# An expert stage's loads moved to SyncE, and one subtraction to GpSimd

## The chip, the cores and the metric

The kernel runs on one core of a Trainium2 chip. The time is that of the device for one launch, in microseconds (us). The core's engines are TensorE (PE; its weight loads are listed as PEld), VectorE (DVE), ScalarE (ACT), GpSimd (POOL) and SyncE (SP), each with its own instruction stream, joined by semaphores. A transfer (DMA) is issued by an engine's queue and done by 16 DMA engines that all queues share.

## The reference

Eight images of 256 channels and 1024 positions go through three layers. The first two are attentions with eight heads; the third, which the change touches, is a layer of 32 experts, computed densely: every expert for every token, with a weight that is zero for all but a token's two best experts.

```python
sel = jax.nn.sigmoid(xt @ expert_sel.T)
sel_val, sel_idx = jax.lax.top_k(sel, TOP_K)                  # TOP_K = 2
w = jnp.zeros((T, E)).at[jnp.arange(T)[:, None], sel_idx].add(sel_val)
h = jax.nn.relu(jnp.einsum('td,edh->teh', xt, keys))          # E = 32, d = 256, H = 64
out = jnp.einsum('teh,te,ehv->tv', h, w, values)
t = t + out.reshape(B, S, -1)
```

## The kernel before

The work is a list of steps per image, written out by hand in `Steps`; every engine walks the same list and does its own part of each step. The sections are `first`, `head`, `body` (a loop of seven) and `last`. The body computes image n's two attentions and, at its beginning, the expert layer of image n-1, its steps spread among the score tiles ("top" steps) of image n. `last` holds the expert layer of the eighth image with nothing beside it. So there are eight expert stages.

All products of this layer are made in float32 accuracy from three float32r products: each operand is split into an upper part (a cast on ScalarE) and a lower part (the value minus its upper part).

A stage handles two halves of 512 tokens (`hf`) and, in each, 16 pairs of experts (`j`, `ET = 16`, `EPT = 2` experts of 64 hidden rows make 128 partitions), so m = 16 hf + j runs over 32 "experts" (pairs). For each m:

- `load_expert(m)` brings keys and values, 128 rows of 2 KB, into `expert_sb[:, m % 4]`; `load_gates(m)` brings the two experts' rows of gates, each repeated over 64 partitions, into `gate_bc[:, m % 4]` (in `probs`). Both are issued by GpSimd (L486, L491), in a ring of four.
- ScalarE casts the keys (L806), GpSimd subtracts their lower part (L498), both two experts ahead.
- TensorE makes 6 matmuls of 512 columns into `ps_one` ("up", L540 to L542).
- VectorE makes the gated activation, relu(up) x gate, into `gated` (L1151).
- ScalarE casts it (L931, `gated_hi`) and casts the values (L932); GpSimd subtracts the values' lower part (L498); VectorE subtracts the activation's lower part (`lower`, L970), one expert later: after the gated activation of m+1.
- TensorE makes 6 matmuls of the values with the activations into `ps_acc`, two experts later (`times_down`). At each half's end the step "down" adds the sum to `x_res` on VectorE (L1160) and SyncE stores it.

GpSimd's order for expert m is: lower part of the keys m+2, of the values m, wait for that result, issue weights m+4, wait until the bank of m-1 was read, issue gates m+3. The two waits are these:

```python
if m + RING < NH * ET:
    hold(vals_down, "up", m + 1)
    load_expert(m + RING)
if 1 <= m and m - 1 + RING < NH * ET:
    b, n = sec.bank(("up",) + divmod(m - 1, ET))
    hold(bank_read[b], b, n)
    load_gates(m - 1 + RING)
```

The gates come from the step "logits" (VectorE), are turned by TensorE ("turn"), copied to `w_turn` (L1141), stored by SyncE to DRAM (`gates_dram`, eight transfers, L435) and only then loaded back. SyncE's other work is the stacks (L424: queries and keys copied into the attention's layout, 12 transfers for each "stack" step), the next image's load and the stores of the output. In the body, between "logits" and "turn", there is one group of stacks; another comes just before "logits". A score tile costs TensorE two matmuls (L657) and VectorE one maximum over 1024 columns (L1055).

Of the kernel before, what the change touches and what calls it, by code (L numbers as in the profile page):

```python
# [46 lines left out]
class Steps:  # L47
# [49 lines left out]
    def experts_of(self, tops):  # L97

        ups = [("up", hf, j) for hf in range(self.halves) for j in range(self.experts)]
        steps = spread(ups, tops) if tops else ups  # L100
        at = steps.index(("up", 0, self.experts - 1)) + 1
        behind = at + 2 if tops else at
        return steps[:at] + [("lower", 0)] + steps[at:behind] + [("down", 0)] + steps[behind:] + [("lower", 1)]

    def batch(self, experts):
        tops = rows_later(self.top(0, 0, 0) + self.top(0, 0, 1) + self.top(0, 1, 0) + self.top(0, 1, 1))
# [76 lines left out]
def bass_hybrid_kernel(nc: bass.Bass, x, mats, vecs, norm_wb, sel_t, experts, out, w_dram):  # L183
# [76 lines left out]
    with ExitStack() as ctx:  # L260
# [3 lines left out]
        def sem(name):  # L264
            return ctx.enter_context(nc.semaphore(name))
# [57 lines left out]
        ps_acc = ctx.enter_context(nc.psum_tensor("ps_acc", [P, 2, HALF], F32))  # L323

        passed = sem("passed")
        passed_too = sem("passed_too")
        consts = sem("consts")
        fills = sem("fills")
        weights_in = sem("weights_in")
# [44 lines left out]
        def f(ap):  # L374
            return ap.bitcast(F32)
# [12 lines left out]
        @block.sync  # L388
        def _(sp):
            sp.dma_start(x_in[:, :, :], x[0].rearrange("(k p) t -> p k t", p=P)).then_inc(x_loaded, 16)  # L390
            sp.dma_start(probs[:, :, :, :].rearrange("p a g t -> p (a g t)"),
                         mats.rearrange("p m k c -> p (m k c)")).then_inc(weights_in, 16)
            sp.dma_start(bias[:, :, :], vecs).then_inc(weights_in, 16)
            sp.dma_start(gnw[:, :, :], norm_wb).then_inc(weights_in, 16)
            sp.dma_start(sel_w[:, :, :], sel_t).then_inc(weights_in, 16)

            def emit(sec, it):
                def hold(semaphore, kind, n, each=1):

                    sp.wait_ge(semaphore, sec.value(kind, n, each))  # L400
                    sp.sem_inc(passed, 1)

                def read(u):
                    b, n = sec.bank(u)
                    hold(bank_read[b], b, n)

                for s in sec.steps:
                    if s[0] == "stack":
                        _, st, g, hf = s

                        read(("qk", st, g, "q", hf))
                        read(("qk", st, g, "k", hf))

                        if st:
                            hold(acc_read, "acc", sec.no["acc"][("norm", 0, g, NH - 1)])
                        elif g == 0 and sec.name != "first":
                            hold(acc_read, "acc", sec.no["acc"][("norm", 1, g, NH - 1)])
                        elif sec.name == "body":
                            hold(acc_read, "acc", 0)
                        for j in range(G):  # L420
                            rows = slice(HD * j, HD * j + HD)

                            for quad, pair in enumerate(stacked_pairs(j)):
                                sp.dma_start(f(stacks[HD * quad:HD * quad + HD, :, g, j, half(hf)]),  # L424
                                             f(nat[rows, pair, half(hf)])).then_inc(stacked[g][hf][j], 16)
                    if s == ("out", 0, NH - 1, CT - 1):

                        read(s)
                        sp.dma_start(x_in[:, :, :],
                                     x[bass.ds(next_batch(it, B), 1)].rearrange("a (k p) t -> p (a k) t", p=P)  # L430
                                     ).then_inc(x_loaded, 16)
                    if s[0] == "turn":
                        read(s)
                        for i in range(TT):
                            sp.dma_start(w_dram[:, P * i:P * i + P],  # L435
                                         w_turn[E * (i % PH):E * (i % PH) + E, i // PH, :]).then_inc(gates_out, 16)
                    if s[0] == "down":
                        hf = s[1]
                        hold(acc_read, "acc", sec.no["acc"][s])
                        where = out[B - 1:B] if sec.name == "last" else out[bass.ds(it - 1, 1)]  # L440
                        sp.dma_start(where.rearrange("a (k p) t -> p (a k) t", p=P)[:, :, half(hf)],
                                     x_res[:, :, half(hf)]).then_inc(stored[hf], 16)

            run(sp, emit)
            last = Section("last")
            sp.wait_ge(gates_out, last.value("turn", 1, 16 * TT))
            for hf in range(NH):
                sp.wait_ge(stored[hf], last.value("turn", 1, 16))
# [3 lines left out]
        def _(pool):  # L452
# [24 lines left out]
                               channel_multiplier=-1).then_inc(consts, 1)  # L477

            def emit(sec, it):
                def hold(semaphore, kind, n, each=1):  # L480

                    pool.wait_ge(semaphore, sec.value(kind, n, each))
                    pool.sem_inc(passed_too, 1)

                def load_expert(m):
                    pool.dma_start(expert_sb[:, m % RING, :], experts[m % ET]).then_inc(expert_in[m % RING], 16)  # L486

                def load_gates(m):
                    hf, j = divmod(m, ET)
                    row = w_dram[EPT * j:EPT * j + EPT, half(hf)]  # L490
                    pool.dma_start(gate_bc[:, m % RING, :],  # L491
                                   bass.AP(row.tensor, row.offset, [[T, EPT], [0, H], [1, HALF]])
                                   ).then_inc(gate_in[m % RING], 16)

                def lower(m, upper_parts, parts, c, lowered):

                    pool.wait_ge(upper_parts, sec.value("up", m + 1))
                    pool.tensor_tensor(parts[:, 2 + m % 2, :], expert_sb[:, m % RING, c:c + C],  # L498
                                       f(parts[:, m % 2, :]), ALU.subtract).then_inc(lowered, 1)

                for s in sec.steps:
                    if s[0] == "logits":

                        hold(acc_read, "acc", 0)
                        for m in range(RING):
                            load_expert(m)
                    if s[0] == "inputs":
                        pool.wait_ge(acts_hi, sec.value("acts", sec.no["acts"][s]))
                        pool.tensor_tensor(act_lo[:, :, :], xn[:, :, :], f(act_hi[:, :, :]),
                                           ALU.subtract).then_inc(acts_lo, 1)  # L510
                    if s[0] == "turn":
                        for m in range(2):
                            lower(m, keys_up, keys_parts, 0, keys_down)
                        hold(gates_out, "turn", sec.no["turn"][s], 16 * TT)
                        for m in range(RING):
                            load_gates(m)
                    if s[0] == "up":
                        m = s[1] * ET + s[2]
                        if m + 2 < NH * ET:
                            lower(m + 2, keys_up, keys_parts, 0, keys_down)  # L520
                        lower(m, vals_up, vals_parts, C, vals_down)
                        if m + RING < NH * ET:

                            hold(vals_down, "up", m + 1)
                            load_expert(m + RING)
                        if 1 <= m and m - 1 + RING < NH * ET:

                            b, n = sec.bank(("up",) + divmod(m - 1, ET))
                            hold(bank_read[b], b, n)
                            load_gates(m - 1 + RING)  # L530

            run(pool, emit)

# [407 lines left out]
        def _(dve):  # L941
# [12 lines left out]
            def emit(sec, it):  # L954
# [9 lines left out]
                def done(ins, u):  # L964
                    ins.then_inc(bank_read[sec.bank(u)[0]], 1)

                def lower(m):

                    dve.wait_ge(gated_up, sec.value("up", m + 1))
                    dve.tensor_tensor(gated_lo[:, m % 2, :], gated[:, m % RING, :], f(gated_hi[:, m % 2, :]), ALU.subtract).then_inc(gated_down, 1)  # L970

                links = [0]

                def link(ins):
# [12 lines left out]
                for s in sec.steps:  # L987
# [154 lines left out]
                    elif kind == "up":  # L1142
# [1 line left out]
                        m = hf * ET + j  # L1144
                        acc = full(s)
                        r = m % RING
                        dve.wait_ge(gate_in[r], (sec.value("turn", 0) * (NH * ET // RING) + m // RING + 1) * 16)

                        if m >= RING:
                            dve.wait_ge(gated_down, sec.value("up", m + 1 - RING))  # L1150
                        done(dve.scalar_tensor_tensor(out=gated[:, r, :], in0=acc, scalar=0.0,  # L1151
                                                      in1=gate_bc[:, r, :], op0=ALU.max, op1=ALU.mult), s)
                        if j:
                            lower(m - 1)
                    elif kind == "lower":
                        lower((s[1] + 1) * ET - 1)
                    elif kind == "down":
                        hf = s[1]
                        dve.wait_ge(downed, sec.value("up", (hf + 1) * ET))
# [58 lines left out]
```

## Time and profile before

| | |
|---|---|
| median of 3 runs | 4135.63 us (4131.19 to 4144.11) |
| the profiled execution | 4131.6 us, its span 4129.9 us |
| TensorE busy | 3465.9 us, 84% of the span |
| VectorE, ScalarE | 2018.6 us, 1666.6 us |
| GpSimd | 767.5 us |
| mean granted TensorE clock | 0.88 |

The span is the time from the first to the last instruction of one profiled execution; the time beside it is that execution's own. Rows of stretches (Rows 2 below) give start and end, length, busy us and instructions of PE, PEld, DVE, ACT and POOL, then the mean granted clock, the DMA engines' busy share and GB/s; the sums add up stretches.
### The profile page before, as it was taken

The numbers are of one execution on the slowest core, as the hardware profiler recorded it, in microseconds if no ns is written. First come the engines' busy times: TensorE is split into PE (matmuls) and PEld (weight loads), VectorE is DVE, ScalarE is ACT, GpSimd is POOL, SyncE is SP. The second block draws the span as 40 slices with busy tenths as digits, with TensorE's granted clock in tenths as the row PEclk, the third lists the DMA queues.
The fourth block names the chain that finished last, engine by engine and source line by source line (L and its number), as shares of the span: only waits on it lengthen the run. The fifth ranks groups of instructions, "written<-read, shape, count | busy, mean of one in ns | idle before, by whom it ended". The sixth has DMA issues, their size and how long they took to land.

```text
span 4129.9 us, 54399 instructions
## 1 busy us (share of the span) xinstructions
PE 3465.9 (84%) x18386; PEld 1874.5 (45%) x18386; DVE 2018.6 (49%) x2825; ACT 1666.6 (40%) x2604; POOL 767.5 (19%) x1051
## 2 busy tenths in 40 slices
PE   5898789887898878988789888898789987898866
PEld 2344554435534455344554445443454434544444
DVE  6435572355724566245652556434563345733533
ACT  1453335442363423634236342453334543355322
POOL 0000260003500044000530005300152001610035
PEclk7797899988998889979899788997889978999889
DMA  3011440214402143022420224211341113411134
GB/s 92 1 42 31 105 119 15 57 25 110 114 12 52 40 115 97 16 57 51 111 77 16 57 66 112 61 31 42 78 111 49 42 31 90 118 32 41 31 89 117
DMA packets 229742, 263.78 MB, mean 64 GB/s; under 512 B 137424, under 2 KB 139472, under 8 KB 229328
## 3 DMA queue, kind: packets, MB, share of 16 engines
q1 hardware_dynamic: 73808, 124.88, 12.6%
q0 software_dynamic: 155648, 135.17, 12.6%
q8 instruction: 170, 2.79, 0.3%
q14 instruction: 116, 0.95, 0.1%
HBM read 145.80 MB, written 9.44 MB: 38 GB/s over the span
## 4 chain that ended last, share of the span: by engine, by line
PE 51%; DVE 14%; DMA 12%; issue 10%; ACT 7%; SPq 2%; POOL 2%; DVEq 0%; ACTq 0%; POOLq 0%
PE ps_acc L588 9%; DMA probs<-gates_dram 9%; PE ps_two L693 8%; PE ps_acc L597 8%; DVE tops L1055 7%; PE ps_one L540 4%; PE ps_one L542 3%; PE ps_one L541 3%; PE ps_two L657 3%; PE ps_one L693 3%; DMA expert_sb<-experts_dram 3%; POOL nat L498 2%; SPq L424 2%; ACT probs L862 1%; ACT stacks L845 1%
## 5 line engine op out<-in xcount | busy, mean ns | idle before, releaser
L1055 DVE TENSOR_REDUCE tops<-ps_two 128x2 bf16<-128x1024 f32 (+3 forms) x896 | 963.0, 1110 | 414.6 <-PE ps_two L657 245.2
L862 ACT ACTIVATE probs<-ps_two 128x1024 f32<-128x1024 f32 (+1 forms) x704 | 642.7, 961 | 302.3 <-PE ps_two L693 229.1
L657 PE MATMUL ps_two<-stacks 32*128 32x512 f32 (+3 forms) x1792 | 444.1, 522 | 254.2 <-DVE tops L1055 200.1
L486 POOL DMA_DIRECT2D expert_sb<-experts_dram x256 | 142.8, 560 | 2593.6 <-DVE rsum L1069 2459.5
L693 PE MATMUL ps_two<-stacks 97*128 97x512 f32 (+3 forms) x1408 | 469.4, 445 | 61.9 <-ACT probs L862 33.5
L588 PE MATMUL ps_acc<-probs,v_sb 128*32 128x512 f32 (+3 forms) x3584 | 475.4, 605 | 0.0
L597 PE MATMUL ps_acc<-probs,ones 128*32 128x512 f32 (+3 forms) x3584 | 448.5, 574 | 0.0
L806 ACT CAST nat<-expert_sb 128x256 fp32r<-128x256 f32 x256 | 103.1, 405 | 850.2 <-DVE probs L1151 604.7
L498 POOL TENSOR_TENSOR nat<-expert_sb,nat 128x256 fp32r<-128x256 f32 x512 | 376.9, 740 | 371.3 <-ACT nat L806 279.6
L657 PEld LDWEIGHTS ps_two<-stacks 32*128 32x128 f32 x1792 | 178.2, 208 | 546.4 <-DVE tops L1055 307.2
L693 PEld LDWEIGHTS ps_two<-stacks 97*128 97x128 f32 x1408 | 253.8, 199 | 335.4 <-issue 189.6
L1151 DVE SCALAR_TENSOR_TENSOR probs<-ps_one,probs 128x512 f32<-128x512 f32 x256 | 176.3, 689 | 371.1 <-issue 170.1
L1069 DVE COPY rsum<-ps_acc 128x512 f32<-128x512 f32 x64 | 44.2, 690 | 551.8 <-PE ps_acc L597 551.8
L540 PE MATMUL ps_acc<-nat 128*128 128x512 f32 x512 | 225.2, 440 | 68.8 <-DVE nat L970 66.7
L540 PE MATMUL ps_one<-act_hi,nat 128*128 128x512 f32 x512 | 242.7, 474 | 28.5 <-POOL nat L498 28.5
L862 ACT ACTIVATE probs<-ps_one 128x512 f32<-128x512 f32 (+3 forms) x384 | 170.0, 488 | 193.6 <-PE ps_one L697 100.8
L845 ACT CAST stacks<-ps_two 1x1024 fp32r<-1x1024 f32 x128 | 128.6, 1005 | 266.1 <-PE ps_two L674 263.5
L540 PE MATMUL ps_one<-act_hi,w_hi 128*128 128x512 f32 x392 | 179.9, 459 | 45.6 <-DVE act_lo L1037 16.9
L541 PE MATMUL ps_one<-act_lo,nat 128*128 128x512 f32 x512 | 217.6, 425 | 0.0
L542 PE MATMUL ps_one<-act_hi,nat 128*128 128x512 f32 x512 | 217.3, 424 | 0.0
L491 POOL DMA_DIRECT2D probs<-gates_dram x256 | 209.0, 819 | 41.6 <-DMA gates_dram<-w_turn 17.6
L597 PEld LDWEIGHTS ps_acc<-probs,ones 128*32 128x32 f32 x3584 | 114.1, 116 | 223.4 <-issue 216.3
(129 smaller groups left out, 4754.5 us busy)
## 6 DMA issues: line engine op xcount, KB each, us to landing
stacks<-nat SPq DMA_DIRECT2D x792, 128.0 KB, 2.4
expert_sb<-experts_dram POOLq DMA_DIRECT2D x256, 256.0 KB, 5.5
probs<-gates_dram POOLq DMA_DIRECT2D x256, 256.0 KB, 8.7
x_in<-x_in_dram SPq DMA_DIRECT2D x9, 1024.0 KB, 4.9
out_dram<-x_res SPq DMA_DIRECT2D x16, 512.0 KB, 4.2
probs<-mats_dram SPq DMA_DIRECT2D x1, 2048.0 KB, 9.4
gates_dram<-w_turn SPq DMA_DIRECT2D x64, 16.0 KB, 1.6
sel_w<-sel_dram SPq DMA_DIRECT2D x1, 32.0 KB, 8.5
```

The lines of the kernel that those rows point to most:

```text
L491: pool.dma_start(gate_bc[:, m % RING, :], bass.AP(row.tensor, row.offset, [[T, EPT], [0, H], [1, HALF]])).then_inc(gate_in[m % RING], 16)
L498: pool.tensor_tensor(parts[:, 2 + m % 2, :], expert_sb[:, m % RING, c:c + C], f(parts[:, m % 2, :]), ALU.subtract).then_inc(lowered, 1)
L540: pe.matmul(acc, lh, rh, start=start, stop=False)
L541: pe.matmul(acc, lh, rl, start=False, stop=False)
L542: return pe.matmul(acc, ll, rh, start=False, stop=stop)
L588: pe.matmul(ps_acc[HD * j:HD * j + HD, 0, a:HALF], v_sb[:, k, c:c + HD], probs[:, sec.no["mix"][s] % 2, j, a:HALF], start=(k == 0), stop=( ...
L597: mm = pe.matmul(ps_acc[HD * j:HD * j + HD, 1, a:HALF], ones32[:], probs[:, sec.no["mix"][s] % 2, j, a:HALF], start=(k == 0), stop=(k == l ...
L657: mm = pe.matmul(acc[:, HALF * e:HALF * e + n_keys], q_st[rows, g, j, P * i:P * i + P], k_st[rows, g, j, HALF * kh:HALF * kh + n_keys], st ...
L693: mm = pe.matmul(at[:, a:HALF], k_st[0:MID + 1, g, j, P * k:P * k + P], q_st[0:MID + 1, g, j, HALF * hf + a:HALF * hf + HALF], start=True, ...
L862: done(act.activation(probs[:, n % 2, per * i:per * i + per, a:HALF], acc[:, :, a:HALF], ACT.Exp, scale=SCALE), s + (i,))
L1055: done(dve.reduce_max(tops[:, kh, 2 * pr:2 * pr + 2, i], acc[:, :, 0:cols(st, i, kh)], AX_X), s)
L1151: done(dve.scalar_tensor_tensor(out=gated[:, r, :], in0=acc, scalar=0.0, in1=gate_bc[:, r, :], op0=ALU.max, op1=ALU.mult), s)
```

## The change

It has three parts. The loads of weights and gates are issued by SyncE, not by GpSimd, with the waits that they need; in SyncE's order the gates m+3 stand ahead of the wait for the values of m. A gate load is made of two transfers, one for each of the two rows of gates, and what waits for it counts both. The lower part of the gated activation is subtracted by GpSimd, last in its order for an expert, and no longer by VectorE.

```diff
@@ Steps.experts_of
-        return steps[:at] + [("lower", 0)] + steps[at:behind] + [("down", 0)] + steps[behind:] + [("lower", 1)]
+        return steps[:behind] + [("down", 0)] + steps[behind:]
@@ SyncE, emit
+                def load_expert(m):
+                    sp.dma_start(expert_sb[:, m % RING, :], experts[m % ET]).then_inc(expert_in[m % RING], 16)
+                def load_gates(m):
+                    hf, j = divmod(m, ET)
+                    for n in range(EPT):
+                        row = w_dram[EPT * j + n:EPT * j + n + 1, half(hf)]
+                        sp.dma_start(gate_bc[H * n:H * n + H, m % RING, :],
+                                     bass.AP(row.tensor, row.offset, [[0, H], [1, HALF]])
+                                     ).then_inc(gate_in[m % RING], 16)
...
+                    if s[0] == "logits":
+                        hold(acc_read, "acc", 0)
+                        for m in range(RING):
+                            load_expert(m)
+                    if s[0] == "up":
+                        m = s[1] * ET + s[2]
+                        if 1 <= m and m - 1 + RING < NH * ET:
+                            read(("up",) + divmod(m - 1, ET))
+                            load_gates(m - 1 + RING)
+                        if m + RING < NH * ET:
+                            hold(vals_down, "up", m + 1)
+                            load_expert(m + RING)
...
+                        hold(gates_out, "turn", sec.no["turn"][s], 16 * TT)
+                        for m in range(RING):
+                            load_gates(m)
@@ GpSimd, emit
-                def load_expert(m):
-                    pool.dma_start(expert_sb[:, m % RING, :], experts[m % ET]).then_inc(expert_in[m % RING], 16)
-                def load_gates(m):
-                    hf, j = divmod(m, ET)
-                    row = w_dram[EPT * j:EPT * j + EPT, half(hf)]
-                    pool.dma_start(gate_bc[:, m % RING, :],
-                                   bass.AP(row.tensor, row.offset, [[T, EPT], [0, H], [1, HALF]])
-                                   ).then_inc(gate_in[m % RING], 16)
...
                         lower(m, vals_up, vals_parts, C, vals_down)
-                        if m + RING < NH * ET:
-                            hold(vals_down, "up", m + 1)
-                            load_expert(m + RING)
-                        if 1 <= m and m - 1 + RING < NH * ET:
-                            b, n = sec.bank(("up",) + divmod(m - 1, ET))
-                            hold(bank_read[b], b, n)
-                            load_gates(m - 1 + RING)
+                        pool.wait_ge(gated_up, sec.value("up", m + 1))
+                        pool.tensor_tensor(gated_lo[:, m % 2, :], gated[:, m % RING, :], f(gated_hi[:, m % 2, :]),
+                                           ALU.subtract).then_inc(gated_down, 1)
@@ VectorE, emit
-                        dve.wait_ge(gate_in[r], (sec.value("turn", 0) * (NH * ET // RING) + m // RING + 1) * 16)
+                        dve.wait_ge(gate_in[r], (sec.value("turn", 0) * (NH * ET // RING) + m // RING + 1) * 16 * EPT)
...
-                        if j:
-                            lower(m - 1)
-                    elif kind == "lower":
-                        lower((s[1] + 1) * ET - 1)
```

GpSimd's waits and loads at the steps "logits" and "turn" go as well.

## Rows read from the trace of the kernel before

**Rows 1.** The page: the chain of work that ended last, by engine and line.

```profile
PE ps_acc L588 9%; DMA probs<-gates_dram 9%; PE ps_two L693 8%; PE ps_acc L597 8%; DVE tops L1055 7%; PE ps_one L540 4%; PE ps_one L542 3%; PE ps_one L541 3%; PE ps_two L657 3%; PE ps_one L693 3%; DMA expert_sb<-experts_dram 3%; POOL nat L498 2%; SPq L424 2%; ACT probs L862 1%; ACT stacks L845 1%
```

**Rows 2.** Stretches: a body stage, seven body stages, seven starts, last start, last stage.

```profile
991.32:1143.86 152.54, 131.10 (x540) 86.05 (x540) 107.29 (x129) 47.50 (x102) 84.08 (x118) 0.91 0.39 104
...
sum 1057.74, PE 914.53 PEld 604.96 DVE 748.07 ACT 332.44 POOL 588.50; mean PE 130.65 PEld 86.42 DVE 106.87 ACT 47.49 POOL 84.07
...
sum 126.46, PE 68.38 PEld 35.43 DVE 52.28 ACT 4.97 POOL 55.41; mean PE 9.77 PEld 5.06 DVE 7.47 ACT 0.71 POOL 7.92
...
3975.72:3990.50 14.78, 4.06 (x12) 2.93 (x12) 0.42 (x1) 0.00 (x0) 3.72 (x5) 0.73 0.22 53
3990.50:4125.20 134.70, 99.13 (x372) 71.92 (x372) 42.84 (x66) 39.04 (x94) 84.75 (x118) 0.94 0.47 117
```

**Rows 3.** The chain in the last stage, in order of time (start, us, what).

```profile
4013.80 0.70 DVE probs L1151
...
4014.53 0.41 ACT nat L806
4014.93 0.52 ACT nat L931
4015.46 0.32 ACT nat L932
...
4015.84 0.74 POOL nat L498
...
4027.04 0.70 DVE probs L1151
```

**Rows 4.** The page's DMA issues: KB each, median us from issue to landing.

```profile
stacks<-nat SPq DMA_DIRECT2D x792, 128.0 KB, 2.4
expert_sb<-experts_dram POOLq DMA_DIRECT2D x256, 256.0 KB, 5.5
probs<-gates_dram POOLq DMA_DIRECT2D x256, 256.0 KB, 8.7
```

**Rows 5.** Timeline of a body step between two gated activations (start, length).

```profile
1049.61 0.68 DVE L1151 SCALAR_TENSOR_TENSOR probs<-ps_one,probs 128x512 f32<-128x512 f32 x1
...
1050.95 2.36 DVE L1055 TENSOR_REDUCE tops<-ps_two 128x2 bf16<-128x1024 f32 x2
...
1051.40 0.40 PE L541 MATMUL ps_one<-act_lo,nat 128*128 128x512 f32 x1
...
1053.22 0.68 DVE L1151 SCALAR_TENSOR_TENSOR probs<-ps_one,probs 128x512 f32<-128x512 f32 x1
...
1053.72 0.39 PE L542 MATMUL ps_acc<-nat 128*128 128x512 f32 x1
```

**Rows 6.** Waits in a body stage: us in total, times, longest.

```profile
ACT nat L806 <- DMA expert_sb<-experts_dram: 24.5, 6, 5.6
DVE probs L1151 <- DMA probs<-gates_dram: 19.8, 8, 10.2
PEld ps_two L657 <- DVE tops L1055: 17.3, 11, 6.8
```

**Rows 7.** The stacks' transfers on SyncE: ns min/median/max of an issue.

```profile
L424 SPq DMA_DIRECT2D stacks<-nat x792: 585/597/1976, 37.0 to 3960.1; - x198
```

**Rows 8.** DMA from 983.2 to 1000, mostly gate loads: packets, queue share.

```profile
DMA packets 2456, 1.59 MB, mean 95 GB/s; under 512 B 2072, under 2 KB 2072, under 8 KB 2456
...
q0 software_dynamic: 2456, 1.59, 35.1%
```

**Rows 9.** DMA from 924 to 930: four weight loads, two stacks.

```profile
DMA packets 319, 1.05 MB, mean 175 GB/s; under 512 B 63, under 2 KB 63, under 8 KB 319
...
expert_sb<-experts_dram POOLq DMA_DIRECT2D x4, 256.0 KB, 3.6
```

**Rows 10.** GpSimd's two subtractions by form: count, busy, mean ns.

```profile
L498 POOL TENSOR_TENSOR nat<-expert_sb,nat 128x256 fp32r<-128x256 f32 x512 | 376.9, 740 | 371.3 <-ACT nat L806 279.6 <-ACT nat L932 73.1
...
L509 POOL TENSOR_TENSOR act_lo<-xn,act_hi 128x2048 fp32r<-128x2048 f32 x8 | 36.0, 4503 | 348.5 <-ACT act_hi L912 348.5
```

More of the change, by code:

```diff
@@ L325, in bass_hybrid_kernel @@
         passed = sem("passed")
-        passed_too = sem("passed_too")
         consts = sem("consts")
@@ L479, in emit @@
             def emit(sec, it):
-                def hold(semaphore, kind, n, each=1):
-                    pool.wait_ge(semaphore, sec.value(kind, n, each))
-                    pool.sem_inc(passed_too, 1)
-                def load_expert(m):
-                    pool.dma_start(expert_sb[:, m % RING, :], experts[m % ET]).then_inc(expert_in[m % RING], 16)
-                def load_gates(m):
-                    hf, j = divmod(m, ET)
-                    row = w_dram[EPT * j:EPT * j + EPT, half(hf)]
-                    pool.dma_start(gate_bc[:, m % RING, :],
-                                   bass.AP(row.tensor, row.offset, [[T, EPT], [0, H], [1, HALF]])
-                                   ).then_inc(gate_in[m % RING], 16)
                 def lower(m, upper_parts, parts, c, lowered):
@@ L501, in emit @@
                 for s in sec.steps:
[L502 to L506, printed above, removed]
                     if s[0] == "inputs":
@@ L513, in emit @@
                             lower(m, keys_up, keys_parts, 0, keys_down)
-                        hold(gates_out, "turn", sec.no["turn"][s], 16 * TT)
-                        for m in range(RING):
-                            load_gates(m)
                     if s[0] == "up":
@@ L965, in done @@
                     ins.then_inc(bank_read[sec.bank(u)[0]], 1)
-                def lower(m):
-                    dve.wait_ge(gated_up, sec.value("up", m + 1))
-                    dve.tensor_tensor(gated_lo[:, m % 2, :], gated[:, m % RING, :], f(gated_hi[:, m % 2, :]), ALU.subtract).then_inc(gated_down, 1)
                 links = [0]
```

## The prediction

> **What bounds the kernel now.** I read the page's chain first, then the time by stage, then the chain inside the expert stage, then the waits and the DMA. The chain of work that ended last is mostly TensorE's lines, but 9% of the span, as much as for any line, go to one kind of transfer, the gate loads (`probs<-gates_dram`), and 3% to the weight loads [rows 1]. The change touches only the expert stages, so the question is how much of the time they are, and what they wait for.
>
> There are eight: seven in the loop body, interleaved with the attention's score tiles ("tops"), and one alone at the end. The seven last 1057.7 us from the first gated activation (L1151) to the first half's output sum, 151.1 us each; the last takes 134.7. Ahead of each lies a start, from the copy of the turned gates (L1141) to that first activation: 126.5 us in seven, 18.1 each, and 14.8 in the last [rows 2]. Together 1334 of 4130 us. TensorE's granted clock is 0.91 in a body stage, a mixture of its two levels, 2.4 and 1.2 GHz. In the last stage VectorE is busy for 43 us of 134.7, GpSimd for 85: neither is full, so something is waited for.
>
> What it is shows in one link of the last stage's chain: gated activation m, three copies on ScalarE, GpSimd's subtraction for the values, two issues, the gate load, gated activation m+3. That is 4027.04 - 4013.80 = 13.24 us for three experts, 4.41 per expert; the work in it is 0.70 + 0.41 + 0.52 + 0.32 + 0.74 = 2.7, all else is issuing and landing [rows 3], and a gate load lands 8.7 us after its issue [rows 4]. The weights make a second loop of nearly the same length, over two experts: copies 0.41, 0.52 and 0.32, GpSimd 0.74, about 1.1 to the end of the issue, landing 5.5: 8.6, or 4.3 per expert [rows 3, 4]. Relieving one of the two alone would give little.
>
> A body stage is a mixture. Two gated activations with two tiles between them stand only 3.61 us apart where nothing is late [rows 5]; the mean over the stage is 4.6. In one stage ScalarE stands 24.5 us for weights and VectorE 19.8 for gates (10.2 of that before the first activation), and TensorE 17.3 for VectorE's maxima, which queue behind the late gated activations [rows 6].
>
> **The gate load leaves GpSimd, as two rows.** 256 issues go from GpSimd; 512 come to SyncE, and 256 of the weights. A stack transfer takes SyncE 0.60 us to issue [rows 7], so 1.8 us per expert, under any period here (0.3 each would make 0.9, 1.5 each 4.5). Landing: 8.7 us now for 256 KB; a SyncE transfer of 128 KB, which a row is too, lands in 2.4 [rows 4]. The trace shows no broadcast row on SyncE; bounds are 2.4 and 8.7, and I take 3.0, near the transfer of the same size and queue. What speaks for it: today's gate loads are odd. In a stretch that is mostly gate loads 2072 of 2456 packets are under 512 B [rows 8], and in one with four weight loads and two stacks 63 of 319 [rows 9]. A plain row has no reason for them.
>
> The Trainium skill ("DMA: Bandwidth & Descriptors", Rules for kernel authors) says that an outermost dimension of c < 16 confines a DMA to at most c engines, here two. The 16 engines are busy for 35.1% of that stretch on this queue [rows 8], which two of them could not give (13%): the trace does not agree. By the rule a row would spread over eight times the engines, by the row of the trace it only loses small packets; the sum takes 3.0 either way.
>
> **The order on SyncE.** For expert m SyncE waits for the bank of m-1, issues gates m+3 (two rows), waits for the values' subtraction of m, issues weights m+4. Gates m+3 are now asked for right after the values of m-1, a period earlier: 3 us after gated activation m-1, and with 1.8 of issues and 3.0 of landing that is 7.8 us, wanted after four periods (12 us or more). Even 8.7 would be in time: the gate loop is gone. What is late next is the weight loop, 0.41 + 0.52 + 0.32 + 0.74 + 0.1 + 0.6 = 2.7 plus the landing L, over two experts. L is 5.5 now, but 3.6 where weights go without gates [rows 9]. With L = 3.0 (between 2.4 for half the bytes and 5.5) it is 2.85 per expert; with 5.5 it stays at 4.1. Behind a waiting SyncE stand only more loads and the half's store; the stacks are issued before the stage. The four first weight loads (2.4 us of issues) go between two groups of stacks, while TensorE still computes what the second group copies. Taken as nothing; without that cover 2.4 in each of eight batches, 19 in all.
>
> **The start.** The first gate load lands 8.7 us after its issue; then two issues and a landing, 1.2 + 3.0 = 4.2. I take a gain of 4.3 in each of eight starts (0 to 5).
>
> **The subtraction moves from VectorE to GpSimd.** GpSimd's price for 128x512 is not in the trace: 0.74 us for 256 columns and 4.50 for 2048 [rows 10] make 2.1 ns a column, so 1.28 (between those two ends). GpSimd then needs 0.74 + 0.74 + 1.28 + 0.1 = 2.86 per expert, without issues; VectorE loses one 128x512 subtraction per expert. The lower part comes last in GpSimd's order, behind the next keys' and the values' subtraction, some 2.5 us later after its activation than now. The product that needs it runs two experts later, which hides that; at the two "down" steps nothing does, so +1 us at the first, where tiles follow, and +3 at the stage's end.
>
> **The sum.** Last stage: TensorE goes from one matmul to the next in 0.23 us at full clock (ten steps from 1051.40 to 1053.72 [rows 5]), 12 of them make 2.76; GpSimd 2.86, weights 2.85. With three limits so close I take 3.05: 31 x 3.05 = 94.6, 4.5 for the end, 3 for low clock: 102 for 134.7. Gain 33, with the start 37.
>
> Body stage: TensorE is the bound. A step with two tiles is 3.61; less 2.76, a tile is 0.43. 31 x 2.76 = 85.6; 54 tiles (64 of the plan less the ten ahead of the stage) x 0.43 = 23.2; seven turns of the row maxima, 0.9 each, an estimate from a tile's 0.43 and a wait as long, 6.3; both ends 4: 119. Low clock: at 0.91, 27 us of the stage run at half speed and cost 13.6; with fewer holes I take about half, 7.5. So 126.5 for 151.1: gain 24.6, with the start 28.9. VectorE then has two maxima and the activation in a step, under 3.2 us, and is no bound.
>
> 7 x 28.9 + 37 = 239. The profiled execution took 4131.6 us (its span 4129.9), 4.0 below the median of 4135.6; 4131.6 - 239 = 3893, and with half of those 4 us about 3895.
>
> **Rivals.**
> *A. The landings stay as they are:* latency belongs to the transfer, not to the issuing engine. Gates at 8.7 fit into four periods anyway; weights at 5.5 hold the loop at 4.1. The last stage keeps its 4.2 (134.7 less 4.5 for the end, over 31), a body stage goes from 4.6 to some 4.35 per expert (31 x 0.28 = 9 us), the starts gain nothing: 7 x 9 = 63, so 4072. Against it: 3.6 for weights without gates [rows 9]. The Trainium skill (same page, Issuing engines are not separate DMA queues) says that another issuing engine saves only the sequencer's time to issue; by itself it leads here.
> *B. The body gives half back.* The clock stays at 0.91 and the maxima pace the step: 12 us less per stage instead of 24.6. 7 x 16.3 + 37 = 151: 3984. For it: VectorE's order is fixed, and TensorE stands 17.3 us for maxima [rows 6].
> *C. Slower: a row costs as much as a whole gate load.* If each row keeps the small packets, the weights wait behind two loads on the same queue instead of one. One gate load more is 8.7 - 5.5 = 3.2, so L = 8.7 and the weight loop (2.7 + 8.7) / 2 = 5.7 per expert: +1.1 in the body, +1.5 at the end, 31 x (7 x 1.1 + 1.5) = 285: 4420. It decides from L = 6.5 on, where the loop passes 4.6.
> *D. No change:* A's 63 us are eaten by SyncE's issues (19 us for the first loads, the rest in the starts).
>
> **How the numbers follow.** Forecast 0.70, A 0.12, B 0.10, C 0.05, D 0.03. The forecast's own range is 3820 (35 us a stage, with TensorE always at full clock and nothing lost at the ends: 7 x 39.3 + 41 = 316) to 3965 (16 a stage and 3 a start: 7 x 19 + 37 = 170). The range of 8 in 10 holds the forecast and B and goes a little beyond on both sides: 3790 to 4035. Within 0.3% (12 us) is what a measurement of this kernel can hardly tell from no change. Faster 0.91 (forecast, B, most of A), same 0.03, slower 0.06.
>
> **What would show it.** Gate rows landing under 4 us and weights near 3; VectorE's waits for gates and ScalarE's for weights nearly gone; GpSimd's 128x512 near 1.28; starts of 14 us, body stages of 125, the last of 102. It is wrong if weights still land in 5.5 us (A) or in over 6.5 (C), if GpSimd's subtraction takes over 2 us, so that GpSimd needs 3.6 per expert and bounds the stage, or if the clock in the stages stays at 0.91 (B).

## The result and the profile after

The changed kernel takes 3913.45 us (median of 4, 3909.43 to 3918.68) against 4133.61 us (median of 4): a ratio of 0.9461, 95% interval 0.9442 to 0.948. The forecast was 3895 us. The profiled execution's span is 3912.4 us, 217.5 less than before.

The same stretches as in [rows 2], read from the kernel after: one body stage, the sum over seven body stages, the sum over their seven starts, the last start and the last stage (start and end, length, busy us of PE, PEld, DVE, ACT and POOL, granted clock, DMA engines' share, GB/s). A stage ends where the second half's output sum begins; the prediction calls that sum the first half's.

```profile
957.34:1088.86 131.52, 122.14 (x541) 82.48 (x540) 89.10 (x96) 48.21 (x102) 85.12 (x94) 0.96 0.40 121
...
sum 917.18, PE 852.49 PEld 576.40 DVE 623.63 ACT 337.46 POOL 595.97; mean PE 121.78 PEld 82.34 DVE 89.09 ACT 48.21 POOL 85.14
...
sum 94.63, PE 66.86 PEld 35.78 DVE 52.34 ACT 4.99 POOL 32.92; mean PE 9.55 PEld 5.11 DVE 7.48 ACT 0.71 POOL 4.70
...
3802.93:3811.87 8.94, 4.17 (x12) 2.99 (x12) 0.42 (x1) 0.00 (x0) 0.50 (x1) 0.85 0.21 65
3811.87:3907.79 95.92, 89.61 (x372) 70.83 (x372) 23.43 (x35) 39.53 (x94) 84.11 (x94) 0.96 0.55 166
```

| | before | after | gain | forecast |
|---|---|---|---|---|
| seven body stages | 1057.7 | 917.2 | 140.6 | 172 |
| seven starts | 126.5 | 94.6 | 31.8 | 30 |
| last stage with its start | 149.5 | 104.9 | 44.6 | 37 |
| sum | 1333.7 | 1116.7 | 217.0 | 239 |

The whole gain lies in the stretches that the change touches; the rest of the span moved by 0.5 us. A body stage is now 131.0 us, where 126.5 were forecast, with TensorE's granted clock at 0.96 to 0.97 instead of 0.91. The last stage takes 95.9, where 102 were forecast.

The queue that now carries everything (share of 16 engines) and its transfers (KB each, median us from issue to landing), from the page; compare [rows 4]:

```profile
q1 hardware_dynamic: 151632, 259.15, 24.6%
...
stacks<-nat SPq DMA_DIRECT2D x792, 128.0 KB, 2.4
expert_sb<-experts_dram SPq DMA_DIRECT2D x256, 256.0 KB, 2.8
probs<-gates_dram SPq DMA_DIRECT2D x512, 128.0 KB, 3.0
```

Weights land in 2.8 us for 5.5, a row of gates in 3.0 for 8.7. In the body stage at 957, VectorE waits for gates once, before the first activation, and TensorE's loads wait for maxima for 5.4 us in all; [rows 6] had 19.8 and 17.3, and 24.5 for weights, a wait that this stage no longer shows (waits: us in total, times, longest). The last stage still has 39.3 us of it on ScalarE, in 24 pieces (36.8 in 11 before): the weight loop is nearly as long as TensorE's period there, as the forecast had it, and no longer decides.

```profile
DVE probs L1144 <- DMA probs<-gates_dram: 5.6, 1, 5.6
PEld ps_two L655 <- DVE tops L1048: 5.4, 5, 2.1
```

GpSimd's timeline in the last stage (start, length). It goes without a gap from one subtraction to the next and repeats every 2.65 us, from 3834.27 to 3836.92; TensorE's own twelve matmuls take 2.72, and 21 of the 31 steps between two gated activations of this stage take that:

```profile
3834.27 1.44 POOL L510 TENSOR_TENSOR nat<-expert_sb,nat 128x256 fp32r<-128x256 f32 x2
3835.66 1.30 POOL L527 TENSOR_TENSOR nat<-probs,nat 128x512 fp32r<-128x512 f32 x1
3836.92 1.44 POOL L510 TENSOR_TENSOR nat<-expert_sb,nat 128x256 fp32r<-128x256 f32 x2
```

The 128x512 subtraction takes 1.29 us, as the forecast of 1.28 had it.

Where a body stage is longer than forecast is seen at its end. The timeline of all engines there:

```profile
1076.94 0.68 DVE L1144 SCALAR_TENSOR_TENSOR probs<-ps_one,probs 128x512 f32<-128x512 f32 x1
...
1079.55 1.26 POOL L527 TENSOR_TENSOR nat<-probs,nat 128x512 fp32r<-128x512 f32 x1
1079.63 1.20 DVE L1054 TENSOR_TENSOR tops<-tops 128x8 bf16<-128x8 bf16 x1
...
1080.89 0.61 PE L672 MATMUL ps_two<-minus_bf,tops 128*1 128x128 bf16 x8 [2.63 <-DVE tops L1054]
...
1083.61 0.63 PE L538 MATMUL ps_acc<-nat 128*128 128x512 f32 x1
...
1088.30 0.52 PE L540 MATMUL ps_acc<-nat 128*128 128x512 f32 x1
1088.86 0.69 DVE L1149 TENSOR_TENSOR x_res<-ps_acc,x_res 128x512 f32<-128x512 f32 x1 [8.03 <-PE ps_acc L540]
```

The last gated activation starts at 1076.94, the output sum at 1088.86: 11.9 us. First TensorE stands 2.63 us for VectorE's maximum over a few columns (L1054), which takes 1.20 us in place of 0.17 and ends 0.02 us after GpSimd's subtraction (L527) beside it. Then come the last twelve products, 5.2 us, with a busy time of 0.63 each: they run at 1.2 GHz, the lower of the clock's two levels, all but the last. So it is, or nearly so, in four of the seven stages; in the other three only the first five run slowly, and the end takes 10.6 to 10.8 us. Slow products at this place are not new: in the kernel before three to twelve of the twelve ran so.

### The profile page after: what moved, and what is told of

Read it like the earlier page. It is cut to its first block, busy times and chain, and to the rows that moved or that the text cites. A ratio compares the mean times of both kernels' runs of the same rounds, so it can differ in the third digit from the quotient of the medians.

```text
span 3912.4 us, 54774 instructions
## 1 busy us (share of the span) xinstructions
PE 3391.0 (87%) x18386; PEld 1846.1 (47%) x18386; DVE 1875.7 (48%) x2569; ACT 1672.8 (43%) x2604; POOL 730.9 (19%) x795
## 3 DMA queue, kind: packets, MB, share of 16 engines
q1 hardware_dynamic: 151632, 259.15, 24.6%
## 4 chain that ended last, share of the span: by engine, by line
PE 68%; DVE 13%; ACT 7%; issue 6%; SPq 3%; DMA 2%; POOL 2%; DVEq 0%; ACTq 0%; POOLq 0%
PE ps_acc L586 10%; PE ps_two L691 8%; PE ps_acc L595 8%; PE ps_one L538 7%; DVE tops L1048 6%; PE ps_two L655 6%; PE ps_one L540 5%; PE ps_one L539 5%; PE ps_one L691 3%; PE ps_acc L538 3%; PE ps_acc L539 3%; PE ps_acc L540 3%; SPq L448 2%; ACT probs L860 2%; PE ps_one L727 2%
## 5 line engine op out<-in xcount | busy, mean ns | idle before, releaser
L655 PE MATMUL ps_two<-stacks 32*128 32x512 f32 (+3 forms) x1792 | 433.0, 515 | 171.0 <-DVE tops L1048 131.4
L516 POOL TENSOR_TENSOR act_lo<-xn,act_hi 128x2048 fp32r<-128x2048 f32 x8 | 36.1, 4508 | 2825.3 <-ACT act_hi L910 2825.3
L527 POOL TENSOR_TENSOR nat<-probs,nat 128x512 fp32r<-128x512 f32 x256 | 329.6, 1288 | 0.0
L538 PE MATMUL ps_one<-act_hi,nat 128*128 128x512 f32 x512 | 232.0, 453 | 22.4 <-POOL nat L510 22.4
L538 PE MATMUL ps_acc<-nat 128*128 128x512 f32 x512 | 211.2, 413 | 9.3 <-POOL nat L527 9.3
L540 PE MATMUL ps_one<-act_hi,nat 128*128 128x512 f32 x512 | 208.4, 407 | 0.0
L539 PE MATMUL ps_one<-act_lo,nat 128*128 128x512 f32 x512 | 208.0, 406 | 0.0
```

The lines of the kernel that those rows point to most:

```text
L527: pool.tensor_tensor(gated_lo[:, m % 2, :], gated[:, m % RING, :], f(gated_hi[:, m % 2, :]), ALU.subtract).then_inc(gated_down, 1)
L538: pe.matmul(acc, lh, rh, start=start, stop=False)
L539: pe.matmul(acc, lh, rl, start=False, stop=False)
L540: return pe.matmul(acc, ll, rh, start=False, stop=stop)
L655: mm = pe.matmul(acc[:, HALF * e:HALF * e + n_keys], q_st[rows, g, j, P * i:P * i + P], k_st[rows, g, j, HALF * kh:HALF * kh + n_keys], st ...
```

## The experiments

**The subtraction alone** (on the kernel before; its loads stay as they were).

```diff
@@ GpSimd, step "up", last
+    pool.wait_ge(gated_up, sec.value("up", m + 1))
+    pool.tensor_tensor(gated_lo[:, m % 2, :], gated[:, m % RING, :], f(gated_hi[:, m % 2, :]), ALU.subtract)
@@ VectorE, step "up"
-    if j:
-        lower(m - 1)
```

> The kernel before with only the gated activations' lower parts moved to GpSimd (last in its order for an expert); all loads stay on GpSimd in their old form. If the two landings bound the stages, this gains nothing: GpSimd then needs two subtractions of 0.74, one of 1.28, a wait of 0.6 and issues of 0.56 and 0.82, 4.7 us per expert against a period of 4.2 to 4.6, so 4135 to 4200 us. Rival: VectorE's relief is what gave the gain, then 4060 or less.

Measured: 4235.03 us, ratio 1.0227 (1.0203 to 1.0252), slower, and 35 us above the upper end expected, but not in the rival's direction. The chain of the last stage (start, us, what) is GpSimd's alone:

```profile
4099.61 0.83 POOL probs L491
4100.44 1.29 POOL nat L532
4101.73 1.39 POOL nat L498 x2
...
4103.15 0.53 issue
...
4103.69 0.56 POOL expert_sb L486
4104.25 0.83 POOL probs L491
```

From 4099.61 to 4104.25 it is 4.64 us per expert: gates' issue 0.83, subtraction 1.29, two subtractions 1.39, wait 0.53, weights' issue 0.56. That is the 4.7 that was expected. What it does to the stages was put too low: a body stage takes 161.8 us, from 151.1, and the last 154.5, from 134.7. 31 such periods are 144 us, and the body needs 151.7 from its first to its last gated activation, so the rest is lost beside the steady period; where is open. This part of the change is a loss unless the loads leave GpSimd.

**The loads alone** (the changed kernel with the subtraction back on VectorE).

```diff
@@ GpSimd, step "up"
-    pool.wait_ge(gated_up, sec.value("up", m + 1))
-    pool.tensor_tensor(gated_lo[:, m % 2, :], gated[:, m % RING, :], f(gated_hi[:, m % 2, :]), ALU.subtract)
@@ VectorE, step "up"
+    if j:
+        lower(m - 1)
```

> The changed kernel with the subtraction back on VectorE; the loads stay on SyncE, gates in two rows. If the landings were the bound, nearly all of the gain is here. In a body step with two tiles VectorE needs 2 x 1.23 + 0.69 + 0.68 = 3.8 us where TensorE needs 3.6: some 4 us more per body stage, less what the earlier lower part saves at the stage's end (1 to 3): 3910 to 3945 us. Rival: the subtraction is worth a third of the gain or more, then 3985 or more.

Measured: 3906.16 us, ratio 0.9438 (0.942 to 0.9457). This is 4 us below the range expected. All of the gain is in the loads; the rival falls. The up-run, from the first to the last gated activation of a body stage, is 120.2 us, against 119.7 with the subtraction on GpSimd: VectorE's 3.8 us in a two-tile step did not lengthen it. The expectation's "4 us more" is wrong.

**The form of the gate load alone** (the kernel before, gates as two rows, still issued by GpSimd).

```diff
@@ GpSimd, load_gates
-    row = w_dram[EPT * j:EPT * j + EPT, half(hf)]
-    pool.dma_start(gate_bc[:, m % RING, :], bass.AP(row.tensor, row.offset, [[T, EPT], [0, H], [1, HALF]]))
+    for n in range(EPT):
+        row = w_dram[EPT * j + n:EPT * j + n + 1, half(hf)]
+        pool.dma_start(gate_bc[H * n:H * n + H, m % RING, :], bass.AP(row.tensor, row.offset, [[0, H], [1, HALF]]))
```

> The kernel before with only the form of the gate load changed: two rows for each expert, still issued by GpSimd. If the small packets belong to the three-level pattern, they vanish, gates land in 3 to 4 us and weights near 3.6; then GpSimd is the bound, 1.48 + 0.6 + 0.56 + about 1.3 for two issues = 3.9 us per expert: 4020 to 4060 us. Rival: the small packets belong to GpSimd's way to issue, then landings stay or get worse, 4130 us or more.

Measured: 3958.55 us, ratio 0.9572 (0.9553 to 0.9591), 61 us below the range expected. Its page, GpSimd's queue (packets, MB, share) and its two loads:

```profile
q0 software_dynamic: 45056, 134.27, 10.8%
...
expert_sb<-experts_dram POOLq DMA_DIRECT2D x256, 256.0 KB, 3.1
probs<-gates_dram POOLq DMA_DIRECT2D x512, 128.0 KB, 3.1
```

The queue had 155648 packets before, for the same data: 432 fewer per expert now. The two loads land in 3.1 us each, and 177 of the 220 us are won with no transfer moved. Only the last stage (119.1 us, 3.7 per expert) is still far from the changed kernel's 95.9. GpSimd fills it: two subtractions of 0.75, a wait of 0.55, an issue of 0.57 and two of 0.53 are 3.7. The body's own pace in the changed kernel is 3.9 us per expert (119.7 over 31), so GpSimd's 3.7 need not bound it there, which fits a time below the range.

**The old form issued by SyncE** (the changed kernel, gates as one transfer again; the subtraction stays on GpSimd).

```diff
@@ SyncE, load_gates
-    for n in range(EPT):
-        row = w_dram[EPT * j + n:EPT * j + n + 1, half(hf)]
-        sp.dma_start(gate_bc[H * n:H * n + H, m % RING, :], bass.AP(row.tensor, row.offset, [[0, H], [1, HALF]]))
+    row = w_dram[EPT * j:EPT * j + EPT, half(hf)]
+    sp.dma_start(gate_bc[:, m % RING, :], bass.AP(row.tensor, row.offset, [[T, EPT], [0, H], [1, HALF]]))
```

> The changed kernel with only the form of the gate load changed back: one transfer for both rows, three-level pattern, issued by SyncE. If the form was the cause of slow landings, gates land in 6 us or more, weights behind them in 4 or more, and the time is 3960 to 4100 us. Rival: the issuing engine alone was the cause, then gates land in about 3 us and the time is that of the changed kernel, 3905 to 3920, with a third fewer issues.

Measured: 4506.3 us, ratio 1.0891 (1.0865 to 1.0918), slower than the kernel before and far above the range expected. Weights now land after 9.8 us (page, DMA issues):

```profile
expert_sb<-experts_dram SPq DMA_DIRECT2D x256, 256.0 KB, 9.8
```

and in the last stage, while only gates move, the share of the 16 engines is 0.13 at about 50 GB/s (stretches of 1 us; the last two columns):

```profile
4357.00:4358.00 1.00, 0.12 (x1) 0.00 (x0) 0.56 (x1) 0.00 (x0) 0.00 (x0) 1.00 0.13 49
4358.00:4359.00 1.00, 0.00 (x0) 0.00 (x0) 0.13 (x1) 0.91 (x3) 0.42 (x1) 1.00 0.13 49
4359.00:4360.00 1.00, 0.65 (x3) 0.56 (x4) 0.00 (x0) 0.32 (x2) 0.90 (x2) 1.00 0.13 51
```

0.13 of 16 is two engines. 256 KB at 50 GB/s are 5.2 us, and the weights of the same queue wait behind them. An estimate from this rate: if the weights spread over all 16 engines, each of the two has 128 KB of gates and 16 KB of weights to move per expert, at 25 GB/s 5.9 us; the period is 6.0. The Trainium skill's rule that an outermost dimension of c confines a DMA to at most c engines ("DMA: Bandwidth & Descriptors", Rules for kernel authors) agrees with this run on SyncE, to the number.

It agrees with the kernel before as well, against the prediction's reading of [rows 8]. There, on GpSimd's queue, the share is 0.12 at 49 GB/s while one gate load moves, 0.27 at 98 while two do, and 0.45 at 135 in the last start, after four were issued in a row:

```profile
4000.50:4001.50 1.00, 1.00 (x6) 0.84 (x5) 0.53 (x1) 0.79 (x2) 1.00 (x2) 1.00 0.12 49
4004.00:4005.00 1.00, 1.00 (x6) 0.61 (x4) 0.00 (x0) 0.00 (x0) 0.44 (x2) 1.00 0.27 98
3988.00:3989.00 1.00, 0.00 (x0) 0.00 (x0) 0.00 (x0) 0.00 (x0) 0.00 (x0) 0.50 0.45 135
```

So one load has about two engines in either kernel, and the 35.1% of [rows 8] are several loads in flight at once. What differs is how several go together. From GpSimd they add up; four issued in a row from SyncE, in the last start of this run and behind it, stay at the rate of one (first row). Rows, in the last start of the changed kernel, use half of the engines (second row):

```profile
4306.00:4318.00 12.00, 4.70 (x11) 3.78 (x12) 1.39 (x2) 1.99 (x5) 2.96 (x4) 0.57 0.13 51
3809.50:3811.00 1.50, 0.00 (x0) 0.00 (x0) 0.00 (x0) 0.00 (x0) 0.00 (x0) 1.00 0.50 179
```

That is why the old form is slower still on SyncE, and why rows help on both queues: of the 5.6 us between landings of 8.7 and 3.1, most would be the 5.2 of moving 256 KB at two engines' rate, an estimate from these rows. The small packets of GpSimd's loads went away together with that, so no run prices them alone.

**Weights on SyncE, gates on GpSimd in the old form** (the subtraction on GpSimd).

```diff
@@ SyncE, step "up" (and the same at "turn")
-    read(("up",) + divmod(m - 1, ET))
-    load_gates(m - 1 + RING)
@@ GpSimd, step "up", after the values' lower part (and the same at "turn")
+    hold(bank_read[b], b, n)
+    load_gates(m - 1 + RING)
```

> The changed kernel with the gates back on GpSimd in their old form, one transfer for both rows; the weights stay on SyncE. Theory: what makes weights land late is the gate loads' packets on the same DMA engines, so another queue helps little: weights land in 4 to 5.5 us, gates in 8 to 9, and the gate loop of 13 us for three experts stays (GpSimd has no weight issue and no wait for it, less 1.1, but may queue the subtraction): 4.1 to 4.4 us per expert, 4080 to 4150 us. Rival: weights were late only because they queued behind the gates on GpSimd's queue; then they land in 2.8 and only the gate loop is left, 3.9 to 4.1 per expert, 4020 to 4070 us.

Measured: 4102.43 us, ratio 0.9923 (0.9899 to 0.9947), within the range expected and outside the rival's. The two loads (page, DMA issues):

```profile
expert_sb<-experts_dram SPq DMA_DIRECT2D x256, 256.0 KB, 5.1
probs<-gates_dram POOLq DMA_DIRECT2D x256, 256.0 KB, 9.0
```

Weights on a queue of their own still take 5.1 us. So they were not late because they stood behind the gates in GpSimd's queue; what the two loads still share is the DMA engines. The 33 us under the kernel before mix two things: this run has the subtraction on GpSimd too. Against that change alone (4235.03) it is 133 us faster, about 0.5 per expert, and what it takes off GpSimd is a wait of 0.53 us and an issue of 0.56 for each. So the issuing engine's time is worth something where that engine is full, but it does not mend the landings.

**Gates asked for later** (the changed kernel with SyncE's waits in the old order).

```diff
@@ SyncE, step "up"
+    if m + RING < NH * ET:
+        hold(vals_down, "up", m + 1)
+        load_expert(m + RING)
     if 1 <= m and m - 1 + RING < NH * ET:
         read(("up",) + divmod(m - 1, ET))
         load_gates(m - 1 + RING)
-    if m + RING < NH * ET:
-        hold(vals_down, "up", m + 1)
-        load_expert(m + RING)
```

> The changed kernel with SyncE's two waits in the old order: weights m+4 first, then gates m+3, so the gates are asked for a period later. Theory: with a landing of 3.0 the gates come in time in either order (asked for some 3 us after gated activation m, wanted 8 us or more after it), so 3905 to 3925 us, no difference. Rival: asking earlier is what freed the gates, then VectorE waits for gates again and the time is 3950 or more.

Measured: 3919.04 us, ratio 0.9491 (0.9443 to 0.9539): no difference from the changed kernel (3913.45 and, below, 3924.41). The earlier asking is worth nothing once a row lands in 3.0 us.

**The changed kernel again, and the loads alone again**, measured beside the two kernels below.

> The changed kernel itself, beside the next kernel on one chip, for the price of the subtraction's place. Theory: with the loads mended, TensorE bounds the stages and the subtraction's engine is worth nothing: within 10 us of the next kernel. Rival: VectorE's relief is worth its 4 us per body stage, then this is 25 us or more faster than the next.

> The changed kernel with the subtraction on VectorE, again, 3900 to 3915 us by the theory that its engine is worth nothing; 3940 or more by the rival.

Measured: 3924.41 us, ratio 0.9491 (0.9459 to 0.9523), and 3896.2 us, ratio 0.9431 (0.9396 to 0.9465). With the subtraction on VectorE the kernel was the faster one both times, by 7 and by 28 us; the intervals touch, so its size is not settled. The theory's "within 10 us" held the first time and missed the second, and the rival, a gain by VectorE's relief, is excluded. The profiles say where a part of the loss lies: a body stage's end, from the last gated activation to the second half's sum, takes 9.3 us against 11.5 (means over seven). In the kernel with the loads alone the maximum at the end is short again (timeline, start and length):

```profile
1083.15 0.17 DVE L1056 TENSOR_TENSOR tops<-tops 128x8 bf16<-128x8 bf16 x1
1083.26 0.69 DVE L964 TENSOR_TENSOR nat<-probs,nat 128x512 fp32r<-128x512 f32 x1
...
1083.38 0.61 PE L669 MATMUL ps_two<-minus_bf,tops 128*1 128x128 bf16 x8 [1.60 <-DVE tops L1056]
```

0.17 us here, 1.20 above, and TensorE waits 1.60 us for it instead of 2.63. GpSimd has no subtraction beside it here, and in the kernel after it ends within 0.02 us of GpSimd's subtraction. The Trainium skill ("SBUF — State Buffer", SBUF: two separate sides) says that a VectorE instruction with two inputs in SBUF and a GpSimd instruction that reads SBUF take the same port in turns, whole instructions long; the two traces agree.

**The second half's sum earlier** (the changed kernel; then the same with the subtraction on VectorE).

```diff
@@ Steps.batch
-        steps += a[:1] + ([("down", 1)] if experts else []) + a[1:]
+        steps = steps[:-1] + ([("down", 1)] if experts else []) + steps[-1:]
+        steps += a
```

In the second kernel VectorE's last lower part (the step "lower", 1) goes ahead of that last row of maxima too.

> The changed kernel with one step moved: the second half's output sum stands ahead of the last row of maxima, not behind it and the next attention's first product. At a body stage's end TensorE stands 2.6 us for a maximum and 1 us for a copy, and then runs the last twelve products at the lower clock, 5.1 us, while nothing else is ready. If this wait and its slow products are what the prediction missed at the stage's end, they go: 3 to 5 us in each of seven stages, 3880 to 3895 us. Rival: the products then wait for GpSimd's last subtraction in the same place, no gain: 3905 to 3918.

> The same step moved, with the subtraction on VectorE. The last lower part is ready some 2.5 us sooner there, so if the rival of the run before is right, this one gains more: 3870 to 3885 against 3905; if not, both are within 10 us.

Measured: 3885.05 us, ratio 0.9393 (0.9357 to 0.9428), and 3876.12 us, ratio 0.9367 (0.9336 to 0.9398). The end of a body stage in the first of them (timeline, all engines):

```profile
1081.60 0.68 DVE L1145 SCALAR_TENSOR_TENSOR probs<-ps_one,probs 128x512 f32<-128x512 f32 x1
...
1085.54 0.19 PEld L539 LDWEIGHTS ps_acc<-nat 128*128 128x128 f32 x1 [1.47 <-POOL nat L528]
...
1087.13 0.61 PE L673 MATMUL ps_two<-minus_bf,tops 128*1 128x128 bf16 x8
1087.23 0.69 DVE L1150 TENSOR_TENSOR x_res<-ps_acc,x_res 128x512 f32<-128x512 f32 x1 [1.73 <-PE ps_acc L541]
```

From the last gated activation at 1081.60 to the sum at 1087.23 are 5.6 us, where the changed kernel beside it needs 11.5; the last six products start after a wait of 1.05 us and run at full clock (0.50 and less each; the granted clock of the stage is 0.99). That is 5.9 us in each of seven stages, 41 us; the medians differ by 39. A wait for GpSimd's last subtraction exists, as the rival said, but it is 1 us. The two are 9 us apart with intervals that overlap, and their ends take 5.6 and 5.2 us, so the earlier lower part is worth little if anything. The second is the fastest kernel here, 6.3% under the kernel before. Why the clock stays up is open. The shorter wait alone does not explain it: in the loads alone, run again, TensorE waits the same 1.60 us in all seven stages, and five to eight of the twelve products are slow in five of them and none in two.

## Why the prediction was right

**The bound was two landings, as said.** The form of the gates mends both at once (3958.55 us), weights on a queue of their own mend neither (4102.43), and gate loads that all share two engines' rate make the kernel slower than before (4506.3).

**The landing of 3.0** was measured as 3.0 for gates and 2.8 for weights. The number was right, the reason for it was not. The small packets do go with the old form (155648 packets became 45056), but the load was slow because one such load has two engines' rate, 49 GB/s. I had set the Trainium skill's rule of two engines aside, because 35.1% of the engines were busy in [rows 8]; that stretch has five gate loads and two weight loads in it, and I had not looked at one alone. The sum survived because the change splits the rows and because 3.0 was taken from the nearest transfer of that size, which was good luck in part. The weight that the prediction gave to "SyncE" was misplaced too: of 220 us, 177 belong to the form, and a row lands as soon from GpSimd (3.1) as from SyncE (3.0).

**The order on SyncE** was costed rightly at nothing, and its early gates are worth nothing. Rivals A and B fell by the landings and by the granted clock, 0.96 to 0.97 where B needed 0.91. A was right that the landing does not hang on the issuing engine; what it missed is that the transfer itself changes. Rival C's mechanism, weights behind two slow gate loads, did not come with the rows; it is what one transfer on SyncE does: with L = 9.8 its loop, (2.7 + 9.8) / 2, is 6.2 us per expert, and 6.0 were measured.

**The subtraction** was priced rightly (1.28 against 1.29) and GpSimd's period slightly too high: 2.65, not 2.86, since two subtractions of 256 columns in a row take 1.44 in all. So most steps of the last stage came to TensorE's own 2.72. Its run from the first to the last gated activation took 89.6 us, low clock and the stop between the halves included, where 94.6 and 3 were forecast; its end took 6.3 for 4.5. Together 6 us more gained than forecast. For the move as a whole I had nothing as a gain and 1 and 3 us as losses at the halves' ends; the runs show no gain and, at the stage's end, 2 us.

**The term that was mis-sized** is the body stage's "both ends 4". It holds only what the moved subtraction adds, 1 and 3, as if the ends took nothing else. The end alone, from the last gated activation to the sum, is 11.4 us (mean over seven); it was 10.0 before, and I had not read it. The rest fits: 85.6 + 23.2 + 6.3 and 7.5 for the clock make 122.6, and the run from the first to the last gated activation took 119.7. So 7.4 too little at the ends and 2.9 too much before them are the 4.5 us per stage, 31 in seven, by which the body fell short; the last stage and the starts gave 9 back. That the rest fits so well is luck too. The granted clock of that run was 0.986, which costs 1.7 us and not 7.5, so the three other terms, 115.1, stand against 118.0 and are 2.9 too small. The end, at a granted clock of 0.77, lost another 2.7.

## What to carry to other kernels

When several loads share the DMA engines, look at the engines' busy share while the oddest of them moves alone, before moving anything to another queue: over a stretch with several loads in flight the share hides how few engines each has. A pattern with a short outermost dimension can slow all loads beside it, and splitting it costs one more issue. Moving work to an idle engine pays only if its old engine was a bound; here it was not, and a large subtraction on GpSimd made small VectorE instructions wait. When a loop's period is forecast, read also what stands between its last turn and the next stage: that end does not shrink with the period.

## What the hardware showed beside that

One load with the three-level source pattern used 0.12 to 0.13 of the 16 DMA engines at about 50 GB/s from either queue. Several from GpSimd in flight together reached 98 and 135 GB/s, several from SyncE stayed at 51; GpSimd's came with over 400 more packets each than rows do, SyncE's did not (its queue has 143952 in all, the changed kernel's 151632). An instruction on VectorE over 8 columns took 1.20 us instead of 0.17 beside GpSimd's 128x512 subtraction. And twelve matmuls after a wait of 2.6 us, with a few other products and a copy between, ran at 1.2 GHz to nearly their end, 5.2 us, in four stages of seven and for the first five in the other three, while after a wait of 1.05 us the last six ran at full clock in all seven.
